# A four-layer graph network on one core: where the last head's projections go, when the exponentials run, and a loop over layers written out

## The reference, cut to what matters

```
for i in range(4):
    y = cond_layer_norm(x, cond, s1_w[i], s1_b[i], b1_w[i], b1_b[i])
    q, k, v = y @ wq + bq, y @ wk + bk, y @ wv + bv        # 4 heads of 128
    scores = einsum('ehd,ehd->eh', q[src], k[dst])         # over the edges
    attn = softmax of scores over the edges of each src
    x = x + segment_sum(attn * v[dst], src) @ wo + bo
    y = cond_layer_norm(x, cond, s2_w[i], s2_b[i], b2_w[i], b2_b[i])
    x = x + relu(y @ m_w1 + m_b1) @ m_w2 + m_b2
```

## Time and profile before

| what | us |
|---|---|
| runs shown: median of 3 (lowest to highest) | 2031.95 (2030.65 to 2033.86) |
| the profiled execution, its own time | 2027.8 |
| its span, first to last instruction | 2026.0 |
| PE busy in the span | 1789.0 |
| DVE busy | 1324.8 |
| ACT busy | 899.6 |
| POOL busy | 392.0 |

### The profile page before, as it was taken

One profiled execution on the slowest core, in us unless ns is written; L12 is line 12 of the kernel. 1 busy time (PEld: TensorE's weight loads), 2 busy tenths in 40 slices (PEclk: granted clock), 3 DMA queues, 4 the chain that ended last, 5 costly groups with the idle time before them and its releaser, 6 DMA issues.

```text
span 2026.0 us, 33390 instructions
## 1 busy us (share of the span) xinstructions
PE 1789.0 (88%) x11835; PEld 1520.1 (75%) x11835; DVE 1324.8 (65%) x2383; ACT 899.6 (44%) x1461; POOL 392.0 (19%) x469
## 2 busy tenths in 40 slices
PE   1566459999999999999999999999999999999898
PEld 0455338888878788888787888887878888878777
DVE  8899955576685555766855557668565576685744
ACT  2798534454454244544542445445323454453221
POOL 5322223000024230000242300002523000023301
PEclk9999879999999999999999999999999999999999
DMA  1300352242231022422310224223102242232122
GB/s 23 109 0 0 127 213 74 80 142 87 85 121 48 17 70 83 141 89 83 122 48 17 66 86 135 95 82 118 52 15 75 81 131 90 91 115 83 39 67 74
DMA packets 62759, 165.81 MB, mean 82 GB/s; under 512 B 5777, under 2 KB 23986, under 8 KB 62605
## 3 DMA queue, kind: packets, MB, share of 16 engines
q10 hardware_dynamic: 23040, 102.41, 15.2%
q1 hardware_dynamic: 39572, 61.45, 9.5%
HBM read 146.58 MB, written 17.02 MB: 81 GB/s over the span
## 4 chain that ended last, share of the span: by engine, by line
PE 61%; issue 15%; DVE 14%; ACT 6%; DVEq 2%; DMA 1%; ACTq 1%; POOL 0%; POOLq 0%
PE ps L1306 55%; PE ps L1488 4%; DVE PT_lo L1094 3%; ACT PT_hi L702 3%; ACT prob L691 2%; DVE prob L1078 2%; PE ps L1408 2%; DVEq L939 1%; DVE CW L950 1%; DVE x L1108 1%; DVE CW L953 1%; DVE onehot L911 1%; DVE CW L997 1%; PE ps L1679 0%; DVE cpart L900 0%
## 5 line engine op out<-in xcount | busy, mean ns | idle before, releaser
L1094 DVE TENSOR_TENSOR PT_lo<-ps,PT_hi 128x512 fp32r<-128x512 f32 x400 | 271.0, 688 | 33.0 <-ACT PT_hi L702 16.2
L691 ACT ACTIVATE prob<-prob,nmax 128x1250 f32<-128x1250 f32 x160 | 214.1, 1338 | 175.6 <-DVE nmax L1078 175.6
L702 ACT ACTIVATE PT_hi<-ps 128x512 fp32r<-128x512 f32 x400 | 231.1, 590 | 70.9 <-PE ps L1488 70.9
L1488 PE MATMUL ps<-ident,prob 128*128 128x128 f32 x1600 | 244.0, 275 | 14.3 <-DVE PT_lo L1094 13.5
L1078 DVE CUSTOM_DVE_ANT_0 prob<-ps,Lr 128x1250 f32<-128x1250 f32 x160 | 232.5, 1453 | 34.5 <-PE ps L1306 31.7
L1306 PE MATMUL ps<-PT_hi,v_hi 128*128 128x256 f32 x800 | 232.9, 291 | 20.2 <-DVE PT_lo L1094 20.2
L1488 PEld LDWEIGHTS ps<-ident,prob 128*128 128x128 f32 x1600 | 184.1, 140 | 67.8 <-DVE PT_lo L1094 47.5
L1306 PE MATMUL ps<-PT_hi,v_lo 128*128 128x256 f32 x800 | 225.8, 282 | 0.0
L1306 PE MATMUL ps<-PT_lo,v_hi 128*128 128x256 f32 x800 | 225.8, 282 | 0.0
L1306 PE MATMUL ps<-k_hi,q_hi 128*128 128x512 f32 (+2 forms) x480 | 191.6, 399 | 0.5
L1306 PEld LDWEIGHTS ps<-PT_hi,v_hi 128*128 128x128 f32 x800 | 152.4, 190 | 33.4 <-DVE PT_lo L1094 33.4
(11 more groups left out here) (209 smaller groups left out, 4106.9 us busy)
## 6 DMA issues: line engine op xcount, KB each, us to landing
Lr<-l_table ACTq DMA_DIRECT2D x160, 625.0 KB, 3.8
piece<-in_L_gnn_m_w_dram SPq DMA_DIRECT2D x32, 256.0 KB, 2.6
w_table<-CW SPq DMA_DIRECT2D x1, 6250.0 KB, 17.7
l_table<-CW SPq DMA_DIRECT2D x10, 625.0 KB, 7.0
prob<-w_table SPq DMA_DIRECT2D x10, 625.0 KB, 4.0
x<-in_x_dram SPq DMA_DIRECT2D x2, 2304.0 KB
piece<-in_L_gnn_wv_dram SPq DMA_DIRECT2D x16, 256.0 KB, 3.0
piece<-in_L_gnn_wq_dram SPq DMA_DIRECT2D x16, 256.0 KB, 4.3
```

The lines of the kernel that those rows point to most:

```text
L691: act.activation(buf, buf, ACT.Exp, bias=nmax[:, i % 4:i % 4 + 1], scale=-1.0, accum_out=rsum[:, i % 4:i % 4 + 1]).then_inc(S["exped"], 1)
L702: act.activation(o, i, ACT.Copy).then_inc(S["pt_hi"], 1)
L1094: dve.tensor_tensor(lo, i, hi.bitcast(F32), ALU.subtract).then_inc(S["pt_split"], 1)
L1488: m = pe.transpose(bank(5 + n % 2, at * P, (at + 1) * P), prob[:, (NT * h + 2 * g + j) % 3, d * P:(d + 1) * P], ident[:])
```

## The change

First, in each group ACT runs exp(i) behind all five evictions in place of between rounds 2 and 3, and exp(i-1) ahead of oT_hi; DVE runs recip of both tiles at the start of the next group. Second, the last group of the last head is written as close(): out_heads of the group before is cut into three parts between the turns, with a new semaphore o_part; tiles 6, 7 and 8 are projected into banks 2, 3 and 4 and tile 9 into 7; hidden(0, 0) and hidden(0, 1) stand ahead of the last projections, and the x adds, centers, norms and statistics of DVE and the rsqrt and last piece of POOL move accordingly. hidden(0) and mlp_out(0) get waits for x_added. Third, job_bank gives the first job bank 4 and the second 7. Fourth, the loop over layers 0 to 2 becomes four written-out layers on every engine.

```
         def job_bank(name):
-            return 7 if name in LATE_VALUES else (7, 4)[JOBS.index(name) % 2]
+            return 7 if name in LATE_VALUES else (4, 7)[JOBS.index(name) % 2]
+        def wo_bank(h, t):
+            return {NT - 4: 2, NT - 3: 3, NT - 2: 4}.get(t, 7) if h == H - 1 else 7
...
         def pieces(h, g, r):
             if h == H - 1 and g == GROUPS - 1:
-                return {0: [MLP1], 1: [MLP1 + 1], 3: [MLP1 + 2], 4: [MLP1 + 3]}.get(r, [])
+                return {0: [MLP1], 1: [MLP1 + 1], 3: [MLP1 + 2]}.get(r, [])
...
-            with sp.Fori(0, LAYERS - 1) as l:
-                layer(l, True)
-            layer(LAYERS - 1, False)
+            for l in range(LAYERS):
+                layer(l, l < LAYERS - 1)
...
# POOL
-                        if h == H - 1 and g:
+                        if h == H - 1 and 0 < g < GROUPS - 1:
                             rsqrt(NT + 2 * g - 2)
                             rsqrt(NT + 2 * g - 1)
+                rest(MLP2 - 1)
                 for n in range(2):
                     rest(MLP2 + n)
-                rsqrt(2 * NT - 2)
-                rsqrt(2 * NT - 1)
                 for c in range(GROUPS):
                     h_rest(c, 0)
                     h_rest(c, 1)
+                    if c < 2:
+                        rsqrt(2 * NT - 4 + 2 * c)
+                        rsqrt(2 * NT - 3 + 2 * c)
...
# ACT
-                    if r == 0:
+                    if h == H - 1 and g == GROUPS - 1:
+                        if r < 2:
+                            wait("o_part", r + 1)
+                        elif r == 2:
+                            wait("o_ready", GROUPS * h + g)
+                    elif r == 0:
                         wait("o_ready", GROUPS * h + g)
...
                         if g:
-                            o_hi_(h, g - 1)
                             exp(i - 1)
+                            if more or not last:
+                                o_hi_(h, g - 1)
                         for r in range(5):
                             pt_hi_(h, g, r)
+                            if last and not more and r == 2:
+                                o_hi_(h, g - 1)
...
-                            if r == 2 and not last:
-                                exp(i)
                             for n in pieces(h, g, r):
                                 piece_hi(n)
+                        if not last:
+                            exp(i)
...
                 y_hi_(NT)
+                piece_hi(MLP2 - 1)
                 y_hi_(NT + 1)
...
# DVE
                         if g:
-                            o_lo_(h, g - 1)
+                            recip(i - 2)
                             recip(i - 1)
+                            if more or not last:
+                                o_lo_(h, g - 1)
...
                             if last and not more:
-                                if r in (0, 3):
-                                    center(NT + r // 3)
-                                if r in (1, 4):
-                                    norm(NT + r // 3)
+                                if r == 0:
+                                    center(NT)
+                                if r == 1:
+                                    norm(NT)
+                                if r == 2:
+                                    o_lo_(h, g - 1)
...
+                add_wo(H - 1, NT - 4)
+                center(NT + 1)
+                norm(NT + 1)
                 y_lo_(NT)
+                add_wo(H - 1, NT - 3)
                 y_lo_(NT + 1)
+                center(NT + 2)
                 o_lo_(H - 1, GROUPS - 1)
-                center(NT + 2)
                 norm(NT + 2)
-                add_wo(H - 1, NT - 2)
-                add_wo(H - 1, NT - 1)
-                for t in (NT - 2, NT - 1):
-                    stats(NT + t)
                 for c in range(GROUPS):
                     if c < GROUPS - 1:
                         for n in (NT + 2 * c + 2, NT + 2 * c + 3):
+                            if n == NT + 2:
+                                add_wo(H - 1, NT - 2)
...
+                        if c == 0:
+                            add_wo(H - 1, NT - 1)
+                        if c < 2:
+                            stats(2 * NT - 4 + 2 * c)
+                            stats(2 * NT - 3 + 2 * c)
...
# PE
-                        wait("x_mlp", 0)
+                        wait("x_mlp", JOBS.index(name) - 1)
...
+                def close():
+                    h, g = H - 1, GROUPS - 1
+                    for r in range(5):
+                        if r < 3:
+                            out_heads(h, g - 1, (range(4), range(4, 8), range(8, NT))[r], range(NT))
+                        turn(h, g, r)
+                        if r in (0, 3):
+                            cond(NT + r // 3)
+                    project(h, g - 1, 0)
+                    project(h, g - 1, 1)
+                    turn_y(NT)
+                    out_heads(h, g, FIRST)
+                    turn_y(NT + 1)
+                    out_heads(h, g, SECOND)
+                    hidden(0, 0)
+                    project(h, g, 0)
+                    turn_y(NT + 2)
+                    hidden(0, 1)
+                    turn_y(NT + 3)
+                    project(h, g, 1)
```

More of the change, by code:

```diff
@@ L601, in _ @@
                 pool.tensor_tensor(lo, raw, hi.bitcast(F32), ALU.subtract).then_inc(S["piece_split"], 1)
-            with pool.Fori(0, LAYERS - 1) as l:
-                layer(l, True)
-            layer(LAYERS - 1, False)
+            for l in range(LAYERS):
+                layer(l, l < LAYERS - 1)
             pool.wait_ge(S["m2_ready"], START + LAYERS * NT)
@@ L797, in _ @@
                 act.activation(yT_hi[:, :, nt(n)], bank(5 + n % 2).rearrange("p (k c) -> p k c", k=KT), ACT.Copy).then_inc(S["y_hi"], 1)
-            with act.Fori(0, LAYERS - 1) as l:
-                layer(l, True)
-            layer(LAYERS - 1, False)
+            for l in range(LAYERS):
+                layer(l, l < LAYERS - 1)
             for t in range(KT):
@@ L1158, in layer @@
                                 recip(i - 1)
-                            if r in (0, 2):
+                            if r in (0, 2) and not (last and not more):
                                 if g:
@@ L1169, in layer @@
                             mask(i + 1)
-                        if g and not more:
+                        if g and not last and not more:
                             stats(NT + 2 * g - 2)
@@ L1219, in _ @@
                 first(0, step)
-            with dve.Fori(0, LAYERS - 1) as l:
-                layer(l, True)
-            layer(LAYERS - 1, False)
+            for l in range(LAYERS):
+                layer(l, l < LAYERS - 1)
             fn = [0]
@@ L1490, in turn, with out_heads @@
                     m.then_inc(S["turned"], 1)
-                def out_heads(h, g, parts):
-                    order = (8, 9, 0, 1, 2, 3, 4, 5, 6, 7)
-                    if 0 in parts:
+                ORDER = (8, 9, 0, 1, 2, 3, 4, 5, 6, 7)
+                FIRST, SECOND = ORDER[:5], ORDER[5:]
+                def out_heads(h, g, tiles, order=ORDER):
+                    if order[0] in tiles:
                         take_m("o_split", GROUPS * h + g + 1)
-                    for d in [d for part in parts for d in order[5 * part:5 * part + 5]]:
+                    for d in tiles:
                         if d in (8, 0, 4):
@@ L1500, in out_heads @@
                                 d == order[0], d == order[-1])
-                    if 1 in parts:
+                    if order[-1] in tiles:
                         m.then_inc(S["o_ready"], 1)
+                    elif order is not ORDER:
+                        m.then_inc(S["o_part"], 1)
                 def project(h, g, j):
                     t = 2 * g + j
-                    take_m("x_added", NT * h + t + 1)
+                    b = wo_bank(h, t)
+                    if b == 7:
+                        take_m("x_added", NT * h + t + 1)
                     if j == 0:
@@ L1511, in project @@
                     cols = slice(j * P, (j + 1) * P)
-                    mm3(bank(7), oT_hi[:, cols], oT_lo[:, cols], wo_hi[:], wo_lo[:], True, True).then_inc(S["wo_ready"], 1)
+                    mm3(bank(b), oT_hi[:, cols], oT_lo[:, cols], wo_hi[:], wo_lo[:], True, True).then_inc(S["wo_ready"], 1)
                 def hidden(c, half_):
@@ L1517, in hidden @@
                         wait("h_relu", n - 1)
+                    else:
+                        wait("x_added", H * NT - 3 + half_)
                     if half_ == 0:
@@ L1534, in mlp_out @@
                         wait("x_mlp", t - 1)
+                    else:
+                        wait("x_added", H * NT - 1)
                     if j == 0:
@@ L1563, in layer @@
                 values(8)
+                wait("v_split", int(JOBS[-1][1]) + 1)
                 scores_a(0, 1, 0)
@@ L1571, in layer @@
```

(34 more changed lines are left out.)

10 lines of the change are left out of this document (4 added, 6 removed).

## The result

| what | before | after |
|---|---|---|
| median of 4 runs each (lowest to highest), us | 2032.51 (2030.65 to 2033.86) | 1965.38 (1964.76 to 1966.29) |
| ratio of times, 95% interval | | 0.9671 [0.9654, 0.9687] |
| the profiled execution, its own time | 2027.8 | 1964.79 |
| its span | 2026.0 | 1963.0 |

The change makes the kernel 67.1 us faster, where 53.9 was forecast; by the spans of the two profiled executions it is 63.0.

What follows compares the result with a forecast made beforehand. PE, busy 1789.0 of 2026.0 us, sets the time; only its gaps can be won. Terms 27.4 + 15.6 + 3.0 + 6.6 + 1.3 = 53.9 off 2027.8 give 1974, plus 4 for the median: 1978; range 1966 to 1994.

Steps and rivals of the forecast that it cites:

- theory A: Posed after the result for the 13 us beyond the forecast: mechanisms are as forecast, and single terms are larger.
- theory B: Posed against theory A: something not in the sum, among them the 4 us of before's runs beyond their profiled execution.
- Exponentials after the evictions: In each group, exponentials behind ACT's evictions remove PE's wait for round 3's low part; 27.4 us kept, bounds 0 and 30.
- 15 x 4 x 0.47: Fifteen groups outside the closing, four layers, a 0.47 us gap by starts before the value products: 28.2 us.
- the closing's walk: Step-by-step count of PE's waits in each layer's last group: eight, 4.55 us by starts, 3.3 idle in place of 7.2.
- So a group becomes 11.06 us and not less: Ordinary group, 11.53 us before: the chain of turn 1, mask, round 2's PT_lo and turn 4 keeps its length.
- The closing: Last group of each layer: reordered products and projection banks cut PE's idle from 7.2 to 3.3 us; 15.6 us in all.
- 3.9 a layer, 15.6 in all: Gain of the rewritten last group through less PE idle; bounds per layer 0 and 6.
- The median of the runs shown is 4 us above it: The runs' median, 2031.95, exceeds the profiled 2027.8 us; this distance was carried over, making 1974 into 1978.
- Banks: At three turns of a layer, v0 in bank 4 no longer waits for add_mlp(9): 3.0 us, bounds 0 and 3.
- Loop: Written-out layers: 6.6 us at the turns into layers 1 and 2, 1.3 us of register waits; bounds 0 and 9.
- rival 3: At layer turns, a taken branch costs next to nothing and the stall stays: 1984.6 us, chance 0.04.

Runs made afterwards that it cites:

- a_noexps: The changed kernel with the old order of exponentials and reciprocals outside the last group of head 3; 2002.12 us, 36.7 us above after.
- u_exps: The kernel before with only the new order of exponentials (ACT) and reciprocals (DVE); 1988.35 us, ratio 0.9795.
- a_noclose: The changed kernel with the old closing of the last head, the rest of the change kept; 1985.68 us, 20.3 us above after.
- u_unroll: The kernel before with the layer loop written out and nothing else; 2028.97 us, ratio 0.9983.
- a_loop: The changed kernel with layers 0 to 2 in a loop again; 1972.81 us, 7.4 us above after.
- u_actonly: The kernel before with only ACT's new order of exponentials, DVE's reciprocal left between rounds 2 and 3; 2164.36 us, ratio 1.0660.

## Why the prediction was wrong, point by point

The mechanisms were those of the forecast, and no rival came; theory A holds for most of the miss. Of the 13.2 us beyond the forecast, 9.1 lie between the two profiled executions and are a matter of the terms: the exponentials' was too small by more than that, and the closing's was too large. The other 4.1 are theory B: the distance between before's runs and its profiled execution, which went away with the change.

**Exponentials after the evictions: right in kind, mis-sized.** The step that failed is "15 x 4 x 0.47". The gap was read from start to start of the two products around the wait, but the next one is late too, by 0.10. Measured: 36.7 us where 27.4 was forecast (35.7 inside the layers), and 39 when the part is put into the kernel before. Of the difference, 6 us are the 60 tenths and 0.8 had been taken off for head 3, where no projection waits. The rest is in the closing, 1.5 us by the layers of a_noexps and more from the side of u_exps, where it is worth 1.15 a layer; the sum had left that wait to the closing's walk. "So a group becomes 11.06 us and not less" fell by the same 0.1: it is 10.97.

**The closing: right in kind, too large, and a clock effect left out.** "3.9 a layer, 15.6 in all" measured 20.3, but not by the walk: at full clock the new closing wins 3.2 to 3.3 a layer, 13 in all (a_noclose). The walk took its 7.2 us of idle from the kernel before; with the new order of exponentials the old closing has 6.6. The idle that is left was forecast well (3.3, measured 3.5); single waits were not: turn_y(11) waited 1.31 us as idle in place of some 0.5, because the piece's landing holds round 4's eviction, and turn 3 only 0.70 by starts in place of 0.95. What the walk left out lies behind the closing: the slow products of hidden(0, 0) or hidden(1, 0) after the old one, some 7 us in the trace of a_noclose. That 20.3 lies above 15.6 is owed to them. I had read layer 1, where the clock stayed at 1.00; the row at 1826.70 in the earlier trace rows, 0.42 us long where the one of layer 1 in the earlier trace rows has 0.28, already showed layer 3 at the lower level.

**"The median of the runs shown is 4 us above it", added to the sum: wrong.** The kernel after has its median 0.6 us above its profiled execution. The runs of before, between 2027.6 and 2040.6 us in the later measurements, go with their mean granted clock: 2027.6 us at 0.984, 2040.6 us at 0.975. a_noexps, with the old waits and the new closing, keeps 0.984 to 0.985 and stays within 1.5 us. u_unroll and a_noclose, with the old closing, go down to 0.979 and 0.980. So the wide spread is seen only with the old closing, and it went with it. The closing alone does not make all of it: u_exps and u_unroll, which keep it, spread over 7 and 6 us in 5 and 12 runs, a_noclose over 5 in 5, before over 13 in more. That the unprofiled runs of before hold the same slow products as the traces of u_unroll and a_noclose is argued from their clock and time, as they have no trace.

**Banks:** 3.0 forecast, 3.1 measured. **Loop:** 7.9 forecast, 7.4 measured in the kernel after, and so rival 3 did not come. Nor was a turn worth the whole 3.66 us of the earlier trace rows: in a_loop it was 2.38 us where no slow products followed. The forecast had no term for layer 0, which reaches its scores 1.2 us later without the loop. Alone the part gave 3.2 only (u_unroll): straight code met the slow products in layers 0 to 2, and layer 0 reached its scores 2.2 us later. The terms don't add up from the side of the kernel before. From the other side they do: 36.7 + 20.3 (with its part of clock) + 3.1 + 7.4 = 67.5, against 67.1.

**Open.** Why the looped layers have a clock of 1.00 behind the old closing in the traces of before and u_exps, and the straight code with the same closing a lower one (u_unroll, a_noclose), no run here tells; it is one trace of each. Why layer 0 reaches its scores 1 to 2 us later without the loop is open too.

## What to carry to other kernels

Measure a wait from the last product at full pace before it to the first at full pace behind it, not only to the one that waited. If two queues share a chain, as exponential and reciprocal do, move both halves or none. Before a profiled execution's distance from the median is carried over, compare the granted clocks of the runs: where they differ, ask which stretch the change will take that distance out of. Compare the kernels of single parts stretch by stretch, and not only by their totals: the total of u_exps came as expected while one of its terms was wrong.

## What the runs showed of the hardware that was not expected

- The second product behind a wait starts 0.22 us after the first (843.66, 843.88) where the pace is 0.12; 60 such waits came to 0.10 us more each.
- Behind 30 to 31 us in which PE was idle for 7, its products ran 0.21 us apart at a granted clock of 0.50, at once or ten us later, in some layers and at 1.00 in others of the same execution; with 3.5 of 26.7 idle, in none of the traces. Each such stretch cost 1.5 us. The runs of the kernel before lie between 2028 and 2040 us with mean clocks of 0.984 to 0.975.
- With a wait of 1.9 us in each group of 13.15 us (u_actonly), 28 stretches at the lower clock came up within four layers; with waits of 0.3 in each group of 11.54 (a_noexps), none did.
- A taken branch of PE's queue took 3.66 and 3.77 us, and the stall behind it was 1.77 to 2.19 us with no releaser. Behind one of the stalls of 2.2 us in a_loop the clock was at 1.00, behind the other at its lower level.
